# Differential attention in half-sequence units: values stationary against 512 transposed differences in float32, part of the routing on GpSimd

## Chip, cores and metric

One NeuronCore of one Trainium2 chip runs the whole layer. The metric is the device time of one execution in microseconds, the median over the runs.

## The reference

A transformer layer on x of 8 sequences x 1024 tokens x 512 features, in float32. First differential attention, then a routed expert layer with 64 experts; each is added to its input and normalised.

```python
q, k = rope(x @ wq.T), rope(x @ wk.T)        # 8 half-heads of width 64
v = x @ wv.T                                 # 4 heads of width 128
probs = softmax(q @ k.T / 128**-0.5)         # two maps of 1024 x 1024 for each head
diff = probs[:, :, 0] - lam * probs[:, :, 1]
attn = diff @ v
attn = attn * rsqrt(mean(attn**2) + eps) * subln_weight
x = layernorm(x + attn @ wout.T)
scores = softmax(x @ gate_w.T); gate_vals, idx = top_k(scores, 6)
# every expert takes at most 128 (CAP) tokens, in order of the token number
x = layernorm(x + routed_experts(x, idx, gate_vals) + shared_expert(x))
```

## The kernel before

The kernel has four stages that run one after the other: `project` (q, k, v and the rotation), `attend`, `experts` and `finish`. The change touches the first two.
`project` writes q, k and v with both parts to DRAM. For the values ScalarE copies the high part out of PSUM (L200) and VectorE subtracts it to get the low part (`v_low`, L217).

`attend` goes over 256 steps. A step is one head of one batch and one tile of 128 query rows; there are 32 steps a batch, 8 tiles x 4 heads. In every step TensorE makes two score maps of 128 x 1024 (L496, L497: the stationary operand holds both parts of q, the moving ones are the high and low part of k). VectorE takes the negated row maxima (L709). ScalarE takes the exponentials with their sums (L627). VectorE combines both maps into `diff` (L666). TensorE turns `diff` in eight pieces (L507, plain float32 transposes). The turned differences leave PSUM in two parts: the high part by ScalarE (L583), the low part of the first four pieces by VectorE (L672), and for the last four TensorE subtracts the high part inside PSUM by a product with minus the identity (L535), after which ScalarE copies the rest (L602). The value product has the turned differences as the stationary operand, 128 x 128, and the values as the moving one, 256 columns (both parts): 16 matmuls a step (L525, L526). ScalarE copies the half with the low part (L599), VectorE adds the two (L642) and ScalarE squares the result for the norm (L609).

Every engine works in turns, one turn for each step. In one turn TensorE issues scores of step j, the transposes of j-2, one of four pieces of output work, and the value product of j-3. Each engine takes its instructions strictly in this order and waits at semaphores. The two score maps have one buffer each, so scores of step j+1 wait for the exponentials of step j.

The output work of the batch before runs beside it, one tile of 128 tokens in four turns ("pieces", `pe_piece`, L544). Piece 0 turns the normed heads. Piece 1 is the output projection, 12 matmuls of 512 columns, after which VectorE adds x and takes the moments (L684 to L689). GpSimd turns these into scale and shift (L798 to L803, four narrow operations), ScalarE applies them (L575) as the first thing of the turn of piece 2, and TensorE turns the result (L560). Piece 3 is the gate product, 12 matmuls of 64 columns, and the exponentials of the logits (L613). The routing of a tile then takes place in the next four turns, a few small VectorE instructions in each turn (`dve_route`, L711): the six best experts (L726, L730), the mask of hits (L736), its sum over the six (L742, L745), the position in each expert's list by two small matmuls (L541, L542), and the slot number (L754 to L767).

GpSimd's queue for one tile (`pool_tiles`, L792) is strictly in this order: scale and shift of tile n, `pool_hit_pos` of tile n-1 (L814), the norm of the heads of tile n+1 (L780 to L790), and `pool_scatter` of tile n-1 (L816), six indirect DMAs that write token and gate value to the slots. It then waits until they have landed.

After the last batch, a tail of 32 turns has output work alone, 8 tiles. The first batch has no output work beside it. The batches 1 to 7 are one hardware loop.

## Time and profile before

| | |
|---|---|
| median of the timed runs | 3913.32 us (3910.45 and 3916.2) |
| span of the profiled execution | 4009.9 us |
| mean granted clock of TensorE | 0.935 |
| TensorE busy, of the span | 3462.3 us (86%) |
| VectorE busy | 2606.1 us (65%) |
| ScalarE busy | 1993.6 us (50%) |
| GpSimd busy | 1442.9 us (36%) |
| HBM | 375.19 MB read, 185.54 MB written |

The profiled execution is longer than the timed ones. Its timeline is what durations are read from. In it `project` runs from 0 to about 540 us, `attend` from there to about 2560 us, and the experts and the last norm take the rest. A busy share is an average over stages with different limits. An instruction's duration in the profile contains its latency, so that matmuls overlap in the rows; the rate is read from the distance of their starts. In a row of a timeline the last bracket is the idle time of the engine before that instruction and what ended it.

### The profile page before, as it was taken

The numbers are of one execution on the slowest core, as the hardware profiler recorded it, in microseconds if no ns is written. First come the engines' busy times: TensorE is split into PE (matmuls) and PEld (weight loads), VectorE is DVE, ScalarE is ACT, GpSimd is POOL, SyncE is SP. The second block draws the span as 40 slices with busy tenths as digits, with TensorE's granted clock in tenths as the row PEclk, the third lists the DMA queues.
The fourth block names the chain that finished last, engine by engine and source line by source line (L and its number), as shares of the span: only waits on it lengthen the run. The fifth ranks groups of instructions, "written<-read, shape, count | busy, mean of one in ns | idle before, by whom it ended". The sixth has DMA issues, their size and how long they took to land. (4 is left out here: it accounts for less than half of the span.)

```text
span 4009.9 us, 61177 instructions
## 1 busy us (share of the span) xinstructions
PE 3462.3 (86%) x18948; PEld 2965.3 (74%) x18948; DVE 2606.1 (65%) x4553; ACT 1993.6 (50%) x3642; POOL 1442.9 (36%) x1496
## 2 busy tenths in 40 slices
PE   8999969998989989898888985299999999999990
PEld 7888859777777777777777774178887788878870
DVE  6777759888878878888887884244444444444434
ACT  2222228766666666666666661144444344444434
POOL 0000000344343433343443435344454545554442
PEclk9999989999999999999999996599999999999995
DMA  6666675434443433443442421255555555555548
GB/s 241 226 229 225 220 219 115 105 91 104 103 102 88 116 89 87 115 98 78 114 101 78 116 67 48 96 161 153 150 166 166 151 152 156 162 168 144 151 126 342
DMA packets 287215, 563.59 MB, mean 141 GB/s; under 512 B 35744, under 2 KB 102880, under 8 KB 282352
## 3 DMA queue, kind: packets, MB, share of 16 engines
q1 hardware_dynamic: 248624, 493.24, 40.7%
q0 software_dynamic: 36032, 50.60, 7.1%
q10 hardware_dynamic: 2304, 16.78, 1.0%
q8 instruction: 108, 1.77, 0.2%
q14 instruction: 147, 1.20, 0.1%
HBM read 375.19 MB, written 185.54 MB: 140 GB/s over the span
## 5 line engine op out<-in xcount | busy, mean ns | idle before, releaser
L709 DVE TENSOR_REDUCE att_neg_max<-att_ps_s 128x1 f32<-128x1024 f32 x512 | 623.1, 1217 | 181.2 <-PE att_ps_s L497 138.8
L627 ACT ACTIVATE att_prob<-att_ps_s,att_neg_max 128x1024 f32<-128x1024 f32 x512 | 573.6, 1120 | 326.0 <-DVE att_neg_max L709 274.9
L525 PE MATMUL att_ps_o<-att_v,att_diff_hi 128*128 128x256 f32 x2048 | 523.2, 293 | 17.8 <-issue 9.2
L526 PE MATMUL att_ps_o<-att_v,att_diff_lo 128*128 128x256 f32 x2048 | 502.3, 283 | 0.0
L496 PE MATMUL att_ps_s<-att_k_hi,att_q 128*128 128x512 f32 x1024 | 432.6, 423 | 78.0 <-issue 46.0
L1040 POOL TENSOR_TENSOR exp_w_lo<-exp_w_raw,exp_w_hi 128x2816 fp32r<-128x2816 f32 x63 | 401.5, 6373 | 272.9 <-ACT exp_w_hi L1031 272.9
L820 POOL DMA_INDIRECT slots<-att_entry,att_slot x390 | 398.7, 1022 | 248.0 <-DVE att_token L767 131.7
L497 PE MATMUL att_ps_s<-att_k_lo,att_q 128*128 128x512 f32 x1024 | 427.1, 417 | 0.0
L525 PEld LDWEIGHTS att_ps_o<-att_v,att_diff_hi 128*128 128x128 f32 x2048 | 391.9, 191 | 23.9 <-issue 23.4
L526 PEld LDWEIGHTS att_ps_o<-att_v,att_diff_lo 128*128 128x128 f32 x2048 | 393.0, 192 | 0.0
L666 DVE SCALAR_TENSOR_TENSOR att_diff<-att_prob,att_weight 128x1024 f32<-128x1024 f32 x256 | 328.0, 1281 | 5.1
L583 ACT CAST att_diff_hi<-att_ps_t 128x1024 fp32r<-128x1024 f32 x256 | 257.5, 1006 | 101.1 <-remote 94.7
L496 PEld LDWEIGHTS att_ps_s<-att_k_hi,att_q 128*128 128x128 f32 x1024 | 205.0, 200 | 136.4 <-issue 77.8
L507 PEld LDWEIGHTS att_ps_t<-att_ident,att_diff 128*128 128x128 f32 x2048 | 253.7, 148 | 59.2 <-issue 19.7
L507 PE MATMUL att_ps_t<-att_ident,att_diff 128*128 128x128 f32 x2048 | 282.3, 284 | 13.1 <-DVE att_diff L666 6.2
L76 PE MATMUL exp_ps_ab<-exp_x_t_hi,exp_sw_hi 128*128 128x512 f32 x704 | 282.4, 401 | 0.0
L798 POOL TENSOR_TENSOR att_var_eps<-att_mean_var,att_eps_col 128x1 f32<-128x1 f32 x64 | 12.0, 187 | 743.8 <-DVE att_mean_var L689 743.8
L78 PE MATMUL exp_ps_ab<-exp_x_t_hi,exp_sw_lo 128*128 128x512 f32 x704 | 275.5, 391 | 0.0
L77 PE MATMUL exp_ps_ab<-exp_x_t_lo,exp_sw_hi 128*128 128x512 f32 x704 | 275.0, 391 | 0.0
L497 PEld LDWEIGHTS att_ps_s<-att_k_lo,att_q 128*128 128x128 f32 x1024 | 206.7, 202 | 43.6
L1200 DVE TENSOR_TENSOR exp_hid<-exp_ps_ab,exp_silu 128x512 f32<-128x512 f32 x80 | 55.1, 688 | 255.0 <-ACT exp_silu L1169 255.0
L76 PE MATMUL proj_ps_qk<-proj_x_hi,proj_wqk_hi 128*128 128x512 f32 x512 | 200.0, 391 | 14.6 <-DVE proj_wqk_lo L211 14.6
(216 smaller groups left out, 8735.3 us busy)
## 6 DMA issues: line engine op xcount, KB each, us to landing
exp_w_raw<-in_w_t SPq DMA_DIRECT2D x64, 1408.0 KB
att_q<-q_parts SPq DMA_DIRECT2D x132, 256.0 KB
att_k_hi<-k_parts SPq DMA_DIRECT2D x132, 256.0 KB
att_k_lo<-k_parts SPq DMA_DIRECT2D x132, 256.0 KB
att_v<-v_parts SPq DMA_DIRECT2D x33, 1024.0 KB
v_parts<-proj_v_out SPq DMA_DIRECT2D x64, 512.0 KB, 3.4
exp_w_raw<-in_w_t SPq DMA_DIRECT2D x64, 512.0 KB, 3.9
proj_x_raw<-in_x_t SPq DMA_DIRECT2D x17, 1024.0 KB, 7.1
```

The source lines that it names most:

```text
L76: nc.tensor.matmul(out, lhs[0], rhs[0], start=first, stop=False)
L78: return nc.tensor.matmul(out, lhs[1], rhs[0], start=False, stop=last)
L496: nc.tensor.matmul(ps_s[s][:, cols], q_buf[h % 2][:, s, q_cols], k_hi[h % 2][:, s, cols], start=True, stop=False)
L497: last = nc.tensor.matmul(ps_s[s][:, cols], q_buf[h % 2][:, s, q_cols], k_lo[h % 2][:, s, cols], start=False, stop=True)
L507: last = nc.tensor.matmul(ps_t[:, t, :], diff[jl % 2][:, t * P : t * P + P], ident[:], is_transpose=True, start=t <= TILES // 2, stop=t < ...
L525: nc.tensor.matmul(ps_o[:, 0 : 2 * VD], diff_hi[i][:, t, :], v_buf[h % 2][:, t, :], start=t == 0, stop=False)
L526: last = nc.tensor.matmul(ps_o[:, 0 : 2 * VD], diff_lo[i][:, t, :], v_buf[h % 2][:, t, :], start=False, stop=t == TILES - 1)
L627: nc.scalar.activation(prob[s][i][:], ps_s[s][:], ACT.Exp, bias=neg_max[:, s, i : i + 1], accum_out=total).then_inc(exp_done[s], 1)
L666: nc.vector.scalar_tensor_tensor(diff[i][:], prob[1][i][:], weight2[:, i : i + 1], prob[0][i][:], ALU.mult, ALU.add).then_inc(diff_done, 1)
L709: nc.vector.tensor_reduce(neg_max[:, s, i : i + 1], ps_s[s][:], AX.X, ALU.max, negate=True).then_inc(max_done[s], 1)
L820: nc.gpsimd.indirect_dma_start(slots, bass.IndirectOffsetOnAxis(ap=slot[:, c : c + 1], axis=0), entry[:, c, :], None, bounds_check=EXPERTS ...
L1040: engine.tensor_tensor(w13[1][:], w13_raw[:], w13[0][:].bitcast(F32), ALU.subtract).then_inc(w13_lo_done, 1)
```

## The change

- The unit of attention is a "quad": one head of one batch and half of the query rows (four steps of 128 rows). There are 8 quads a batch and again 32 steps. Query loads bring 512 columns and not 1024. Keys are loaded for each quad, so twice as often.
- The turned differences are copied out of PSUM by one ScalarE copy a step into `diff_t`, plain float32. The high and low parts of the differences, their VectorE subtraction, the product with minus the identity and the second ScalarE copy are gone.
- The value product runs once for a quad: eight matmuls, stationary the values (128 keys x 128 features, float32, one part), moving 512 turned differences, float32. They are issued three, two and three in the turns 2, 3 and 0 of the four.
- Its result has features on the partitions. ScalarE copies it out (`out_t`), TensorE turns it back with four transposes, VectorE copies it to `raw`. This takes place in the turn of piece 1.
- `project` writes values in one part; `v_low` is gone.
- Output work of a tile begins 24 turns after the batch's first step (`OUT`), so in the same batch and not one batch later. The tail has 28 turns and holds the output work of 6 tiles.
- In the routing, top values and indices are taken from the exponentials directly, all VectorE work but `pos_k`, the copy of the positions and the running mask sits in the turn of piece 0. The copy of the indices, the three adds that make the mask and all the slot arithmetic are GpSimd instructions.
- GpSimd's order for one tile is now: scale and shift of n, the norm of n+1, `pool_hit_pos` of n-1, `pool_choose` of n, `pool_scatter` of n-1. Two sets of slot buffers take the place of the wait for the landing.

```diff
-    STEPS = HEADS * TILES
+    QT = 4
+    QUADS = 2 * HEADS
+    STEPS = QUADS * QT
+    DIFF, TURN, COPY, VALUE, BACK, SQUARE, OUT, ROUTE = 1, 2, 3, 6, 9, 10, 24, 28
+    VALUE_TILES = [(0, 1, 2), (3, 4), (5, 6, 7)]
...
-        q_buf = [st.sbuf(f"q{i}", [P, 2, SEQ], F32R) for i in range(2)]
+        q_buf = [st.sbuf(f"q{i}", [P, 2, CHUNK], F32R) for i in range(2)]
...
-        v_buf = [st.sbuf(f"v{i}", [P, TILES, 2 * VD], F32R) for i in range(2)]
+        v_buf = [st.sbuf(f"v{i}", [P, TILES, VD]) for i in range(2)]
...
+        diff_t = [st.sbuf(f"diff_t{i}", [P, TILES, CHUNK]) for i in range(2)]
+        out_t = st.sbuf("out_t", [P, CHUNK])
...
+        def pe_turns(pe, b, mode):
+            for jl in turns(mode):
+                piece = jl % QT
+                if live(mode, jl, 0):
+                    pe_scores(pe, b, jl)
+                if piece != 2:
+                    pe_piece(pe, b, jl, mode)
+                if live(mode, jl, TURN):
+                    j = STEPS * b + jl - TURN
+                    pe.wait_ge(diff_done, j + 1)
+                    wait_past(pe, copy_done, j)
+                    for c in range(TILES):
+                        last = nc.tensor.transpose(ps_t[:, c, :], diff[jl % 2][:, c * P : c * P + P], ident[:])
+                    last.then_inc(t_done, 1)
+                if piece == BACK % QT and live(mode, jl, BACK):
...
+                    pe.wait_ge(out_t_done, qn + 1)
+                    for t in range(QT):
+                        last = nc.tensor.transpose(ps_o[:, t * P : t * P + P], out_t[:, t * P : t * P + P], ident[:])
+                    last.then_inc(back_done, 1)
+                i = (jl - VALUE) % QT
+                if i < len(VALUE_TILES) and live(mode, jl, VALUE):
...
+                    for c in VALUE_TILES[i]:
+                        last = nc.tensor.matmul(ps_o[:], v_buf[q % 2][:, c, :], diff_t[q % 2][:, c, :], start=c == 0, stop=c == TILES - 1)
...
+                if piece == 2:
+                    pe_piece(pe, b, jl, mode)
...
+        def act_turns(act, b, mode):
...
+                if piece == BACK % QT and live(mode, jl, BACK):
...
+                    nc.scalar.copy(out_t[:], ps_o[:]).then_inc(out_t_done, 1)
+                if live(mode, jl, COPY):
...
+                    act.wait_ge(t_done, j + 1)
+                    wait_past(act, value_done, qn - 1)
+                    t = (jl - COPY) % QT
+                    nc.scalar.copy(diff_t[q % 2][:, :, t * P : t * P + P], ps_t[:]).then_inc(copy_done, 1)
...
                 if out and piece == 2:
                     act.wait_ge(ln_done, n + 1)
...
                     nc.scalar.activation(x1_buf[k % 2][:], summed[:], ACT.Identity, bias=shift[:], scale=rstd[:]).then_inc(x1_done, 1)
+                if live(mode, jl, 0):
+                    for s in range(2):
+                        exp(act, b, jl, s)
...
         def pool_tiles(pool, b, final):
             for k in range(TILES):
...
                 nc.gpsimd.tensor_tensor(shift[:], neg_mean[:], rstd[:], ALU.mult).then_inc(ln_done, 1)
-                pool_hit_pos(pool, n - 1)
                 if k < TILES - 1:
-                    pool_norm_heads(pool, b - 1, k + 1)
...
+                    pool_norm(pool, n + 1, par, t, STEPS * b + QT * HEADS * par + QT * (HEADS - 1) + t)
...
-                pool_scatter(pool, n - 1)
...
+                if not first:
+                    pool_hit_pos(pool, n - 1)
+                pool_choose(pool, n, k % 2)
+                if not first:
+                    pool_scatter(pool, n - 1, (k - 1) % 2)
...
+        def pool_choose(pool, n, par):
+
+            pool.wait_ge(route_step, ROUTE_STEPS * n + 3)
+            pool.sem_inc(held, 1)
+            nc.gpsimd.tensor_copy(chosen[par][:], top_idx[:, 0:TOPK]).then_inc(chosen_done, 1)
+            pool.wait_ge(hit_step, HIT_STEPS * n + 1)
+            nc.gpsimd.tensor_tensor(hit3[:], hit[:, 0 : TOPK // 2, :], hit[:, TOPK // 2 :, :], ALU.add).then_inc(hit_step, 1)
+            pool.wait_ge(hit_step, HIT_STEPS * n + 2)
+            nc.gpsimd.tensor_tensor(hit2[:], hit3[:, 0, :], hit3[:, 1, :], ALU.add).then_inc(hit_step, 1)
+            pool.wait_ge(hit_step, HIT_STEPS * n + 3)
+            wait_past(pool, seen_done, n)
+            nc.gpsimd.tensor_tensor(mask[:], hit2[:], hit3[:, 2, :], ALU.add).then_inc(mask_done, 1)
...
+            nc.gpsimd.tensor_scalar(over[:], pos_k[:], float(CAP), BIG, ALU.is_ge, ALU.mult).then_inc(slot_step, 1)
+            nc.gpsimd.tensor_scalar(first_slot[:], chosen[par][:], float(CAP), None, ALU.mult).then_inc(slot_step, 1)
+            nc.gpsimd.tensor_copy(entry[par][:, :, 0], token[:].to_broadcast([P, TOPK])).then_inc(token_done, 1)
...
+            nc.gpsimd.tensor_copy(slot[par][:], slot_sum[:]).then_inc(slot_done, 1)
```

In the new order of VectorE, the last routing instruction of the turn of piece 0 makes `hit` (after `diff` of that turn). `pool_choose` waits for it, and `pool_scatter` of the tile before and scale and shift of the next tile are behind `pool_choose` in GpSimd's queue. In the turn of piece 1, VectorE copies `raw` ahead of `diff`, and the sum with x and the moments come after `diff`.

## Rows read from the trace of the kernel before

**Rows 1.** Busy time by stretch: us, busy us of each engine, clock, DMA share
```profile
100.00:500.00 400.00, 400.00 (x1766) 331.23 (x1765) 290.11 (x259) 96.58 (x112) 0.00 (x0) 1.00 0.65 225
...
900.00:1300.00 400.00, 355.49 (x2243) 309.06 (x2243) 331.15 (x708) 258.90 (x555) 161.06 (x214) 0.95 0.41 101
```

**Rows 2.** Timeline of GpSimd: start us, us, engine line op, operands
```profile
748.37 0.19 POOL L798 TENSOR_TENSOR att_var_eps<-att_mean_var,att_eps_col 128x1 f32<-128x1 f32 x1 [10.39 <-DVE att_mean_var L689]
...
949.00 0.19 POOL L798 TENSOR_TENSOR att_var_eps<-att_mean_var,att_eps_col 128x1 f32<-128x1 f32 x1 [10.26 <-DVE att_mean_var L689]
...
2404.85 0.19 POOL L798 TENSOR_TENSOR att_var_eps<-att_mean_var,att_eps_col 128x1 f32<-128x1 f32 x1 [9.10 <-DVE att_mean_var L689]
...
2531.81 0.19 POOL L798 TENSOR_TENSOR att_var_eps<-att_mean_var,att_eps_col 128x1 f32<-128x1 f32 x1 [4.44 <-DVE att_mean_var L689]
...
2556.77 0.97 POOL L820 DMA_INDIRECT slots<-att_entry,att_slot  x1 [0.30 <-issue]
```

**Rows 3.** Timeline of TensorE, parts of two turns
```profile
1485.11 0.39 PE L496 MATMUL att_ps_s<-att_k_hi,att_q 128*128 128x512 f32 x1
...
1486.94 1.03 PE L507 MATMUL att_ps_t<-att_ident,att_diff 128*128 128x128 f32 x8
...
1487.81 0.60 PE L560 MATMUL att_ps_m<-att_ident,att_x 128*128 128x128 f32 x4
...
1488.16 0.36 PE L525 MATMUL att_ps_o<-att_v,att_diff_hi 128*128 128x256 f32 x1
...
1490.15 0.40 PE L535 MATMUL att_ps_t<-att_diff_hi,att_neg_ident 128*128 128x512 f32 x1
...
1493.23 0.28 PE L76 MATMUL att_ps_m<-att_gate_hi,att_x_t_hi 128*128 128x64 f32 x1
...
1494.57 0.36 PE L525 MATMUL att_ps_o<-att_v,att_diff_hi 128*128 128x256 f32 x1
```

**Rows 4.** Group of the row maxima in 590 to 720 us, busy us, mean ns | idle before
```profile
L709 DVE TENSOR_REDUCE att_neg_max<-att_ps_s 128x1 f32<-128x1024 f32 x52 | 63.1, 1214 | 6.9 <-PE att_ps_s L497 6.9
```

**Rows 5.** Timeline of VectorE, two stretches
```profile
1481.83 1.28 DVE L666 SCALAR_TENSOR_TENSOR att_diff<-att_prob,att_weight 128x1024 f32<-128x1024 f32 x1
...
1483.02 0.68 DVE L672 TENSOR_TENSOR att_diff_lo<-att_ps_t,att_diff_hi 128x512 fp32r<-128x512 f32 x1
...
1485.18 0.18 DVE L689 BATCH_NORM_AGGREGATE att_mean_var<-att_stats 128x2 f32<-128x6 f32 x1 [0.15 <-DVE att_stats L686]
...
1499.90 1.22 DVE L709 TENSOR_REDUCE att_neg_max<-att_ps_s 128x1 f32<-128x1024 f32 x1 [2.61 <-remote]
...
1504.26 0.21 DVE L730 FIND_INDEX8 att_top_idx<-att_top_val,att_score 128x8 uint32<-128x64 f32 x1
```

**Rows 6.** Timeline of GpSimd around one tile, and one pause
```profile
1485.45 0.19 POOL L798 TENSOR_TENSOR att_var_eps<-att_mean_var,att_eps_col 128x1 f32<-128x1 f32 x1 [12.24 <-DVE att_mean_var L689]
...
1487.66 1.01 POOL L814 TENSOR_TENSOR att_hit_pos<-att_hit,att_pos 128x384 f32<-128x384 f32 x1 [0.95 <-DVE att_pos L705]
...
1489.27 1.22 POOL L785 TENSOR_TENSOR att_rms_sum<-att_squares,att_eps_mass 128x4 f32<-128x4 f32 x1 [0.17 <-POOL att_eps_mass L782]
...
1494.86 1.08 POOL L820 DMA_INDIRECT slots<-att_entry,att_slot  x1 [1.96 <-DVE att_token L767]
...
1501.55 0.98 POOL L820 DMA_INDIRECT slots<-att_entry,att_slot  x1 [0.30 <-issue]
...
1864.78 0.97 POOL L820 DMA_INDIRECT slots<-att_entry,att_slot  x1 [10.81 <-issue]
```

**Rows 7.** Timeline of ScalarE, three instructions
```profile
1487.65 1.11 ACT L627 ACTIVATE att_prob<-att_ps_s,att_neg_max 128x1024 f32<-128x1024 f32 x1
...
1503.65 1.01 ACT L583 CAST att_diff_hi<-att_ps_t 128x1024 fp32r<-128x1024 f32 x1 [1.20 <-remote]
...
1854.93 1.00 ACT L583 CAST att_diff_hi<-att_ps_t 128x1024 fp32r<-128x1024 f32 x1
```

**Rows 8.** Busy time by stretch, while queries and keys are loaded
```profile
1498.00:1501.00 3.00, 2.11 (x16) 1.70 (x14) 1.09 (x1) 0.28 (x2) 2.39 (x3) 1.00 1.03 200
```

More of the change, by code:

```diff
@@ new lines, in attend, with turns, live, quad @@
+        ROUTE_STEPS, HIT_STEPS, SLOT_STEPS, RMS_STEPS, LN_STEPS = 4, 3, 4, 4, 3
+        SCATTER = DMA * TOPK
+        TILES_ALL = TOKENS // P
+        def turns(mode):
+            return range(ROUTE if mode == "last" else STEPS)
+        def live(mode, jl, lag):
+            return jl >= lag if mode == "first" else jl < lag if mode == "last" else True
+        def quad(b, jl, lag):
+            return QUADS * b + (jl - lag) // QT, (jl - lag) // QT % QUADS
+        def tile(b, jl, lag):
+            at = (jl - lag) // QT
+            return TILES * b + at, at % TILES, TILES // 2 * b + at // 2
@@ new lines, in pe_scores @@
+        def pe_scores(pe, b, jl):
+            q, t, j = jl // QT, jl % QT, STEPS * b + jl
+            if t == 0:
+                pe.wait_ge(qk_in[q % 2], DMA * LOADS_QK * (QUADS // 2 * b + q // 2 + 1))
+            q_cols = slice(t * P, t * P + P)
+            for s in range(2):
+                wait_past(pe, exp_done[s], j)
+                for half in range(2):
+                    cols = slice(half * CHUNK, half * CHUNK + CHUNK)
+                    nc.tensor.matmul(ps_s[s][:, cols], q_buf[q % 2][:, s, q_cols], k_hi[q % 2][:, s, cols], start=True, stop=False)
+                    last = nc.tensor.matmul(ps_s[s][:, cols], q_buf[q % 2][:, s, q_cols], k_lo[q % 2][:, s, cols], start=False, stop=True)
+                last.then_inc(s_done[s], 1)
@@ new lines, in pe_piece @@
+        def pe_piece(pe, b, jl, mode):
+            piece = jl % QT
+            n, k, _ = tile(b, jl, OUT)
+            if piece == 3 and live(mode, jl, ROUTE):
+                pe.wait_ge(mask_done, n)
+                wait_past(pe, seen_done, n - 1)
+                if live(mode, jl, OUT):
+                    pe.wait_ge(xt_lo_done, n + 1)
+                else:
+                    wait_past(pe, score_done, n)
+                nc.tensor.matmul(ps_m[:, POS], before[:], mask[:], start=True, stop=False)
+                nc.tensor.matmul(ps_m[:, POS], ones[:], mask_seen[:], start=False, stop=True).then_inc(pos_done, 1)
+            if not live(mode, jl, OUT):
+                return
@@ L578, in act_turns @@
-                if live[2]:
-                    _, _, _, j2 = of_lag(b, jl, 2)
-                    act.wait_ge(t_done, j2 + 1)
-                    if not (first and jl < 4):
-                        act.wait_ge(o_done, j2 - 1)
-                    nc.scalar.copy(diff_hi[jl % 2][:], ps_t[:]).then_inc(hi_done, 1)
+                if live(mode, jl, 0):
+                    for s in range(2):
+                        exp(act, b, jl, s)
+                if out and piece == 0:
+                    act.wait_ge(at_done, n + 1)
+                    wait_past(act, y_done, n)
+                    nc.scalar.copy(heads_t[0][:], ps_m[:].rearrange("p (h t) -> p h t", t=P)).then_inc(at_hi_done, 1)
@@ L584, in act_turns @@
                 if out and piece == 2:
                     act.wait_ge(xt_done, n + 1)
[L586 removed]
+                    wait_past(act, gate_done, n)
                     nc.scalar.copy(x1_t[0][:], ps_m[:].rearrange("p (h t) -> p h t", t=P)).then_inc(xt_hi_done, 1)
[L588 to L593 removed]
@@ L603, in act_turns @@
-                if live[4]:
-                    bb, h, t, j = of_lag(b, jl, 4)
-                    act.wait_ge(raw_done, j + 1)
-                    if not (first and jl == 4):
-                        act.wait_ge(square_done, j)
-                    par = bb % 2
+                if live(mode, jl, SQUARE):
+                    qn, q = quad(b, jl, SQUARE)
+                    h, par, t = q % HEADS, q // HEADS, (jl - SQUARE) % QT
+                    act.wait_ge(raw_done, qn + 1)
+                    wait_past(act, square_done, STEPS * b + jl - SQUARE)
@@ L879, in _ @@
-                act.wait_ge(weight_step, 1)
-                nc.scalar.copy(wo[0][:], wo_raw[:]).then_inc(setup_act, 1)
-                nc.scalar.copy(gate[0][:], gate_raw[:]).then_inc(setup_act, 1)
+                act_turns(act, 0, "first")
                 with act.Fori(1, BATCH) as b:
-                    act_turns(act, b, True, True, False)
-                act_turns(act, BATCH, False, True, False)
+                    act_turns(act, b, "steady")
+                act_turns(act, BATCH, "last")
```

582 lines of the change are left out of this document (225 added, 357 removed).

## The prediction, made before the changed kernel ran

> **What bounds the kernel now.** I read the busy time by stretch first. `project` is TensorE without a gap, 400 of 400 us [rows 1], VectorE has spare time there. In the steady part of `attend` TensorE has work in 355 of 400 us and VectorE in 331 [rows 1]: two engines near their limit, waiting for each other. So I need the time of one tile (four turns), and what it is made of.
>
> The timeline of GpSimd gives it. The first operation of a tile's scale and shift starts at 748.37 for the first tile and at 949.00 seven tiles later: 28.66 us a tile. Seven batches later it is 2404.85, so 236.6 a batch, of which 8 x 28.66 = 229.3 are tiles and 7.3 the wrap of the loop. The tail then takes (2531.81 - 2404.85) / 7 = 18.1 a tile, and 25.9 us from there to the end of the last scatter at 2557.7 [rows 2]. Without output work a turn takes 130 / 26 = 5.0 us: 52 row maxima, two a turn, in 130 us [rows 4].
>
> What TensorE has to do in one tile follows from starts: scores 1.83 a turn, so 0.229 for a product of 512 columns; transposes 0.87; values 1.99; four more transposes 0.35; gate 1.34 [rows 3]. With the product with minus the identity at 0.229, four turns are 4 x (1.83 + 0.87 + 1.99 + 0.23) = 19.7. The output work adds 12 x 0.229 = 2.75, 1.34 and 2 x 0.35, together 4.8. Sum 24.5 of 28.66: some 4 us a tile are waits.
>
> **TensorE after.** Removed in a tile: 4 x 1.99 and 4 x 0.23, together 8.9. Added: four transposes, 0.35, and eight matmuls of plain float32 with 512 columns, which no row shows. Lower bound: one pass as for the scores, 0.229. I take 0.916: values with one part and differences with one part are only exact enough if the array does the splitting. Then 7.3 are added, and the sum is 24.5 - 8.9 + 0.35 + 7.3 = 23.3.
>
> The Trainium skill's "FP8 and Floating Point Precision", section on TensorE precision notes, says true float32 takes four passes through the array. By it the price is that of my upper bound; by the one pass TensorE would have 17.8 us a tile. No row here can decide.
>
> **The other engines.** VectorE loses the low part (0.60 a turn by the distance to the next start, 0.68 by its row [rows 5]), the add of the halves and the masks. ScalarE loses two copies a turn. Neither is what a turn then waits for by its sum, so I price these removals at nothing themselves. The two waits on TensorE's path they end (scores held by the copy, the product with minus the identity held by the high part) are in the 4 us above. In `project` the removed subtraction lay beside a full TensorE: nothing, about 1 us at the stage's end. The wait of 29 us for the first load gets 0.5 MB less: 2 us.
>
> **GpSimd after, the step that decides.** The queue is in order, so I walk one tile from the moment when VectorE's `hit` is ready (turn of piece 0), called 0. Then, on GpSimd:
> - three adds for the mask, of 192, 64 and 64 columns. 384 columns take 1.0 and a narrow operation 0.19 [rows 6], so 0.6, 0.35, 0.35 with the hand-overs between them: 1.5 with rounding up.
> - seven narrow operations for the slots, 0.2 each: 1.5.
> - six scatters: 1494.86 to 1502.53 [rows 6], 7.7.
> - only then scale and shift of the next tile. That begins at 10.7.
>
> From there to the start of the first exponential it is 1487.65 - 1485.45 = 2.2 [rows 6, 7], the exponential takes 1.1 [rows 7], and at 14.1 TensorE can start scores of the turn of piece 3. Its second map waits for the second exponential, until 15.2, and ends at 16.2. Behind the exponentials ScalarE copies the turned x1 and VectorE makes its low part (0.6 each by the low part in rows 5): 16.4. From there TensorE has work in one piece: gate 1.34, transposes 0.87, two value matmuls 1.83, first score map of the next turn 0.92: 21.4. VectorE needs 1499.90 to 1504.47 = 4.6 from that map's maximum to the index of the top values [rows 5], and 0.5 for `hit`, half of what GpSimd takes for the same 384 columns [rows 6]: 26.5. So 26.5 us a tile.
>
> Without GpSimd in the way, the turn of piece 1 sets the moments: TensorE does scores 1.83, output projection 2.75, transposes 0.87, four back 0.35, so 5.8; VectorE then has `raw`, `diff`, sum, moments. Before, `diff` to the end of the moments was 1481.83 to 1485.36 with the low part in it [rows 5], and `raw` has the size of that part: 3.5. Scale and shift could start at 9.4 and not at 10.7. That would be 25.2 a tile: moving the slots to GpSimd costs 1.3. If the float32 product took one pass, two of them leave the path, but VectorE comes in its place after 0.7: 25.8.
>
> **DMA.** A quad loads 2.5 MB of queries and keys and 0.5 MB of values in one tile's time; before it was 4 MB in two. At the 200 GB/s of such a stretch [rows 8], with 0.75 MB of x in and out, 3.75 MB are 18.8 us of 26.5. The load starts when the scores of the quad before last are done and has over a quad's time to land: hidden.
>
> **A port.** A GpSimd addition of 4 columns took 1.22 us [rows 6] where its like take 0.2; VectorE's `diff`, two inputs from SBUF, is 1.28 long [rows 5]. I read that as a wait for it. In my walk the next `diff` comes at 6.4, behind the masks and slots, so the sum has nothing for it; where it is met it is rival 6. The Trainium skill's "SBUF — State Buffer", section "SBUF: two separate sides", speaks against moving work to GpSimd: a VectorE operation with two SBUF inputs and a GpSimd operation that reads SBUF exclude each other for the whole instruction. The 1.22 us agree with it.
>
> **The sum.** First output tile: 568.1 less 2, some 8 for the slow start, 24 turns at 5.0 - 1.99 - 0.23 + 1.83 + 0.09 = 4.7, so 113, and 13 for turns 24 and 25: 700. Tile 57 is the last with attention beside it: 57 x 26.5 + 7 x 7.3 = 1562 later, 2262. The next, without scores, 24 (before 26 at that place). Five of the tail: a tile's chain there is 18.1; `hit` comes 9.9 after scale and shift begin and GpSimd is busy for 10.7 from there: 20.6, so 103. After the last: 9.9, masks 1.5, slots and scatters 9.2 of tile 62, then positions 1.0 + 0.7, slots 1.5, scatters 7.7: 32. End at 2421 and not 2557.7: 137 us less, in a profiled execution of 4009.9. The timed runs are 3913.3 / 4009.9 = 0.976 of it: -134, so 3780 us.
>
> **The rivals.** All change the time of a tile; one microsecond is 57 x 0.976 = 56 us of the timed run.
> 1. *GpSimd is not late*: 25.2 a tile, 3780 - 72 = 3708. For it: my margin of 1.3 us is thin, two narrow operations less wide would eat half. Against it: six scatters at 1.28 are firm.
> 2. *A copy is held by the scatters.* ScalarE's copy of the turned differences in the turn of piece 0 starts at 1503.65, after 1.2 idle with its releaser unknown, 1.1 after the last scatter's end at 1502.53; in the tile in which the scatters paused for 10.81 us the same copy came without a gap, at 1854.93 [rows 6, 7]. If scatters do hold it, then in the new order the copy of turn 2 (ready at 5.6) is held to 11.8; transposes end at 13.6, three value matmuls at 16.3, turned x1 at 16.7, where scores started at 14.1. A part overlaps with what followed: 2.1 more, 28.6 a tile, 3898: no change.
> 3. *Slower: both copies are held.* The copy of turn 1 starts at 0.7, and the scatters at 3.0. If it comes 2.3 us later it is caught too, the exponentials behind it start at 12.7, scores of the turn of piece 2 at 13.9 and not at 5.9: 8 more, 34.5 a tile, 4228. Against it: it needs those 2.3 us.
> 4. *Slower: the float32 product is dearer.* TensorE's other work is 16.0 a tile, so above (26.5 - 16.0) / 8 = 1.31 it is the bound; the kernel is slower than before from 28.9 a tile, 1.61 each. At 1.83, twice my price, 30.6 a tile: 4010.
> 5. *The loads are not hidden*, if short elements (2 KB for queries, 512 B for values) are slow: needs 1.4 times the 18.8 us. Then the tile is as long as its loads, 27 to 29: 3810 to 3920.
> 6. *Masks or slots meet a `diff`* once in a tile, as the addition of 1.22 us did: 1.2 more, 27.7 a tile, 3847. Against it: `hit` stands right behind a `diff`, with a turn to the next.
>
> **How the numbers follow.** Forecast 0.40, rival 1 0.19, rival 2 0.20, rival 3 0.07, rival 4 0.06, rival 5 0.04, rival 6 0.04. The forecast's own range is 3730 to 3835 (25.7 to 27.5 a tile). The range for 8 in 10 reaches from 3700, rival 1, to 3910, just above rival 2; it leaves out rivals 3 and 4, 0.13, and the edges of others, some 0.07. More than 2% (below 3835, above 3992, about what a measurement can tell from no change) comes out faster in rival 1, nearly all of the forecast and a part of rival 5, 0.60; slower in 3 and 4, 0.13; the rest 0.27.
>
> **What would show it.** Right: the first operation of scale and shift comes 26.5 us apart, straight behind the sixth scatter, and its idle time has no VectorE releaser; float32 value matmuls start 0.92 apart; the x1 operation of ScalarE waits for GpSimd some 3 us a tile; TensorE is busy for about 88% of that stretch. Rival 1: GpSimd idle before scale and shift. Rival 2 or 3: the copy into `diff_t` idle with an unknown releaser while scatters run. Rival 4: value matmuls over 1.3 apart. Rival 5: scores waiting for a DMA. Wrong altogether: a time below 3680, which only a TensorE with less to do and no queue before it could give, or above 4030.

## The result: slower, and the profile after

The changed kernel takes 4152.7 us (4129.4 and 4176.1), against 3913.3: ratio 1.061, 95% interval 1.047 to 1.076. I had forecast 3780 and a range from 3700 to 3910. The span of the profiled execution is 4174.4, 164.5 more than before; here it is close to the timed runs, before it was 97 us above them.

**Stretches.** `project` and the experts are unchanged, `attend` is not. Columns as in [rows 1]: us, busy us of PE, PEld, DVE, ACT, POOL, granted clock, DMA share, GB/s.

```profile
100.00:500.00 400.00, 400.00 (x1767) 331.20 (x1766) 260.83 (x211) 96.88 (x110) 0.00 (x0) 1.00 0.57 193
900.00:1300.00 400.00, 349.49 (x1502) 247.60 (x1501) 261.27 (x463) 219.48 (x438) 188.84 (x348) 0.87 0.55 128
1300.00:1700.00 400.00, 351.32 (x1396) 249.65 (x1395) 239.54 (x422) 200.77 (x400) 176.93 (x313) 0.80 0.51 118
```

TensorE looks as busy as before (349 of 400), with a third fewer matmul records. A part of that busy time is work at the lower clock: 0.87 and then 0.80, where [rows 1] had 0.95. VectorE fell from 331 to 261 and is no limit. DMA is at 0.55.

**The tile.** Scale and shift (now L707), timeline of GpSimd, as in [rows 2]:

```profile
697.22 0.19 POOL L707 TENSOR_TENSOR att_var_eps<-att_mean_var,att_eps_col 128x1 f32<-128x1 f32 x1 [17.72 <-DVE att_mean_var L662]
722.28 0.19 POOL L707 TENSOR_TENSOR att_var_eps<-att_mean_var,att_eps_col 128x1 f32<-128x1 f32 x1 [8.06 <-DVE att_mean_var L662]
750.42 0.85 POOL L707 TENSOR_TENSOR att_var_eps<-att_mean_var,att_eps_col 128x1 f32<-128x1 f32 x1
780.47 0.85 POOL L707 TENSOR_TENSOR att_var_eps<-att_mean_var,att_eps_col 128x1 f32<-128x1 f32 x1
...
1680.48 0.94 POOL L707 TENSOR_TENSOR att_var_eps<-att_mean_var,att_eps_col 128x1 f32<-128x1 f32 x1
1714.62 0.86 POOL L707 TENSOR_TENSOR att_var_eps<-att_mean_var,att_eps_col 128x1 f32<-128x1 f32 x1
...
2561.18 0.84 POOL L707 TENSOR_TENSOR att_var_eps<-att_mean_var,att_eps_col 128x1 f32<-128x1 f32 x1
```

The first four rows hold the case in short. Up to the second row no scatter stands ahead of scale and shift: 25.06 us, and GpSimd is idle until the moments come. Up to the third there are six: 28.14, no idle time. The next distance is 30.05, and later it is 34.14. Over 57 tiles the mean is (2561.18 - 697.22) / 57 = 32.7.

**What stands ahead of scale and shift.** The same timeline, from the end of VectorE's `hit` (1265.66):

```profile
1265.74 0.60 POOL L740 TENSOR_TENSOR att_hit<-att_hit 128x192 f32<-128x192 f32 x1 [1.76 <-DVE att_hit L643]
...
1268.74 0.19 POOL L764 CAST att_slot<-att_slot_sum 128x6 int32<-128x6 f32 x1 [0.17 <-POOL att_slot_sum L761]
1269.79 1.10 POOL L770 DMA_INDIRECT slots<-att_entry,att_slot  x1 [0.86 <-POOL att_slot L764]
1271.19 0.98 POOL L770 DMA_INDIRECT slots<-att_entry,att_slot  x1 [0.30 <-issue]
1272.48 1.80 POOL L770 DMA_INDIRECT slots<-att_entry,att_slot  x1 [0.30 <-issue]
...
1277.14 0.97 POOL L770 DMA_INDIRECT slots<-att_entry,att_slot  x1 [0.30 <-issue]
1278.12 0.85 POOL L707 TENSOR_TENSOR att_var_eps<-att_mean_var,att_eps_col 128x1 f32<-128x1 f32 x1
```

From `hit` to scale and shift pass 12.5 us; I had 10.7. The moments had been ready for 3.0 us (rows of VectorE and ScalarE in the same tile; L565 is ScalarE's operation that makes x1, the normed sum):

```profile
1272.16 1.28 DVE L639 SCALAR_TENSOR_TENSOR att_diff<-att_prob,att_weight 128x1024 f32<-128x1024 f32 x1
1274.95 0.18 DVE L662 BATCH_NORM_AGGREGATE att_mean_var<-att_stats 128x2 f32<-128x6 f32 x1 [0.18 <-DVE att_stats L658]
1277.64 1.28 DVE L639 SCALAR_TENSOR_TENSOR att_diff<-att_prob,att_weight 128x1024 f32<-128x1024 f32 x1
1280.08 0.81 ACT L565 ACTIVATE att_x<-att_summed,att_shift,att_rstd 128x512 f32<-128x512 f32 x1 [7.95 <-POOL att_shift L712]
```

**What TensorE does about it.** Its timeline in that tile, and in one of the longer ones:

```profile
1274.42 2.74 PE L483 MATMUL att_ps_o<-att_diff_t,att_v 128*128 128x512 f32 x6
1281.03 1.09 PE L532 MATMUL att_ps_m<-att_ident,att_x 128*128 128x128 f32 x4 [3.87 <-ACT att_x L565]
1282.03 0.79 PE L498 MATMUL att_ps_s<-att_k_hi,att_q 128*128 128x512 f32 x1
1282.62 0.63 PE L499 MATMUL att_ps_s<-att_k_lo,att_q 128*128 128x512 f32 x1
1283.05 0.63 PE L498 MATMUL att_ps_s<-att_k_hi,att_q 128*128 128x512 f32 x1
...
1649.37 1.09 PE L532 MATMUL att_ps_m<-att_ident,att_x 128*128 128x128 f32 x4 [4.01 <-ACT att_x L565]
...
1658.42 3.62 PE L483 MATMUL att_ps_o<-att_diff_t,att_v 128*128 128x512 f32 x4
1661.06 1.42 PE L498 MATMUL att_ps_s<-att_k_hi,att_q 128*128 128x512 f32 x1
...
1662.78 0.39 PE L499 MATMUL att_ps_s<-att_k_lo,att_q 128*128 128x512 f32 x1
```

After the last three value matmuls TensorE stands for some 4 us, waiting for x1, and then the scores come 0.43 apart where [rows 3] had 0.23. Busy time by stretch of the same two tiles, and of the stretch with which the experiments are compared:

```profile
1281.00:1287.00 6.00, 5.97 (x21) 4.58 (x21) 3.04 (x5) 4.96 (x10) 2.25 (x3) 0.51 0.42 134
1287.00:1306.00 19.00, 18.88 (x97) 14.02 (x97) 13.82 (x29) 11.20 (x23) 8.35 (x16) 1.00 0.79 166
...
1649.00:1662.00 13.00, 12.63 (x39) 9.18 (x40) 4.99 (x9) 8.21 (x18) 3.06 (x3) 0.50 0.64 164
1662.00:1676.00 14.00, 13.85 (x68) 10.42 (x67) 10.39 (x20) 8.39 (x16) 6.05 (x14) 0.99 0.59 131
...
1500.00:2200.00 700.00, 616.09 (x2443) 437.80 (x2444) 423.18 (x743) 355.67 (x705) 311.25 (x559) 0.81 0.50 117
```

The lower level of the clock (1.2 GHz) is granted for 6 us behind the one gap and for 13 behind the other; the rest of the tile runs at 2.4. The tile that began at 1249.81 had a gap of only 0.99 and full clock and took 28.3; these take 30.6 and 34.1. In 6 us at half rate 3 us of work are done, and in 13 us 6.5, so 3 and 6.5 us can be lost; the tiles are 2.3 and 5.8 longer. The Trainium skill's "TensorE: Matmul & The Clock Gate", section on HAM oscillation, describes a matmul kernel in which a wait in each step of a loop sends the clock back to the lower level again and again; this trace agrees, with 0.80 over 1300 to 1700.

So the theory before the experiments: GpSimd's queue makes x1 late; TensorE stands for 4 us; the stall costs a second time, by the clock behind it. The rivals: the float32 value product is what costs, by its length or by drawing the clock down on its own; or GpSimd's work costs wherever it stands.

### The profile page after: what moved, and what is told of

Read it like the earlier page. It is cut to its first block and busy times, and to the rows that moved or that the text cites. A ratio compares the mean times of both kernels' runs of the same rounds, so it can differ in the third digit from the quotient of the medians.

```text
span 4174.4 us, 53729 instructions
## 1 busy us (share of the span) xinstructions
PE 3593.0 (86%) x15874; PEld 2785.7 (67%) x15874; DVE 2274.4 (54%) x3428; ACT 1864.7 (45%) x3194; POOL 1631.2 (39%) x2191
## 5 line engine op out<-in xcount | busy, mean ns | idle before, releaser
L498 PE MATMUL att_ps_s<-att_k_hi,att_q 128*128 128x512 f32 x1024 | 544.9, 532 | 35.4 <-DVE att_neg_lam L836 27.4
L483 PE MATMUL att_ps_o<-att_diff_t,att_v 128*128 128x512 f32 x1024 | 542.3, 667 | 0.9 <-DVE att_raw L635 0.9
L770 POOL DMA_INDIRECT slots<-att_entry,att_slot x384 | 422.8, 1101 | 155.9 <-issue 105.0
L499 PE MATMUL att_ps_s<-att_k_lo,att_q 128*128 128x512 f32 x1024 | 454.6, 444 | 0.0
L483 PEld LDWEIGHTS att_ps_o<-att_diff_t,att_v 128*128 128x128 f32 x1024 | 201.6, 214 | 176.6 <-issue 175.5
L467 PE MATMUL att_ps_t<-att_ident,att_diff 128*128 128x128 f32 x2048 | 307.9, 299 | 12.2 <-DVE att_diff L639 2.7
L556 ACT COPY att_diff_t<-att_ps_t 128x1024 f32<-128x1024 f32 x256 | 259.3, 1013 | 85.6 <-PE att_ps_t L467 56.3
L467 PEld LDWEIGHTS att_ps_t<-att_ident,att_diff 128*128 128x128 f32 x2048 | 256.4, 154 | 50.1 <-DVE att_diff L639 35.3
L532 PE MATMUL att_ps_m<-att_ident,att_x 128*128 128x128 f32 x256 | 66.4, 411 | 250.0 <-ACT att_x L565 250.0
L565 ACT ACTIVATE att_x<-att_summed,att_shift,att_rstd 128x512 f32<-128x512 f32 x64 | 52.0, 812 | 509.0 <-POOL att_shift L712 509.0
L532 PEld LDWEIGHTS att_ps_m<-att_ident,att_x 128*128 128x128 f32 x256 | 43.7, 209 | 299.5 <-issue 299.5
```

Of the source, the lines that this page charges most:

```text
L467: last = nc.tensor.transpose(ps_t[:, c, :], diff[jl % 2][:, c * P : c * P + P], ident[:])
L483: last = nc.tensor.matmul(ps_o[:], v_buf[q % 2][:, c, :], diff_t[q % 2][:, c, :], start=c == 0, stop=c == TILES - 1)
L498: nc.tensor.matmul(ps_s[s][:, cols], q_buf[q % 2][:, s, q_cols], k_hi[q % 2][:, s, cols], start=True, stop=False)
L499: last = nc.tensor.matmul(ps_s[s][:, cols], q_buf[q % 2][:, s, q_cols], k_lo[q % 2][:, s, cols], start=False, stop=True)
L770: nc.gpsimd.indirect_dma_start(slots, bass.IndirectOffsetOnAxis(ap=slot[par][:, c : c + 1], axis=0), entry[par][:, c, :], None, bounds_che ...
```

## The experiments

Line numbers are those of each kernel; they are up to five higher than those of the changed one. All ratios are to the kernel before. Clocks are those of the stretch from 1500 to 2200 us, sums of waits those from 1350 to 2300 (for experiment 10 from 1500 to 2200).

**1. The scatters one tile later** (`e1_scatter_late`). GpSimd's order is scale and shift, heads, slots and scatters of two tiles ago, `hit_pos`, masks:

```diff
+                late = not (isinstance(b, int) and n < 2)
+                if late:
+                    pool_scatter(pool, n - 2, k % 2)
                 if not first:
                     pool_hit_pos(pool, n - 1)
+                if late:
+                    pool.wait_ge(scattered[k % 2], SCATTER * (TILES // 2 * b + (k - 2) // 2 + 1))
+                    pool.sem_inc(entry_free, 1)
                 pool_choose(pool, n, k % 2)
-                if not first:
-                    pool_scatter(pool, n - 1, (k - 1) % 2)
...
```

> All work is done; the six scatters of a tile and their slots are issued one cycle later on GpSimd, behind the scale of the heads (L699), so that the scale and shift (L707) follows the masks directly. Theory (queue): in the changed kernel L707 starts 3.0 us after VectorE's moments, behind the sixth scatter; here it starts right behind the moments. TensorE's idle time before L532 falls from 3.7 us a tile to under 1.5, its granted clock in 1500:2200 rises from 0.81 to 0.95 or more, a tile takes 25 to 26.5 us and not 30.7 to 34.1, and the time is 3700 to 3850. Rival A (the float32 value product lowers the clock by itself): the tile gets only the 3.0 us, the clock stays at 0.80 to 0.85, time 3950 to 4000. Rival B (the float32 product or the DMA is the bound): idle time moves elsewhere, time 4050 to 4150.

4346.9 us, ratio 1.113 (1.109 to 1.117): the slowest of all, 35.3 us a tile. No expectation named this. Scale and shift does follow the moments (GpSimd is idle for 9.7 us ahead of it), and something else is late:

```profile
1690.11 1.04 POOL L732 TENSOR_TENSOR att_hit_pos<-att_hit,att_pos 128x384 f32<-128x384 f32 x1
1696.81 0.23 DVE L628 TENSOR_SCALAR att_entry<-att_top_val,att_score_inv 128x6 f32<-128x6 f32 x1 [8.31 <-POOLq L725]
...
1696.99 0.23 POOL L738 CAST att_chosen<-att_top_idx 128x6 f32<-128x6 uint32 x1 [5.84 <-DMA slots<-att_entry,att_slot]
```

Entries have two buffers. VectorE may write the next one when the scatters of two tiles ago have landed, and I had just put those scatters in front of it. VectorE stands for 8.3 us in the middle of its turn. In the changed kernel's own order that release had been free.

**2. TensorE kept busy in the gap** (`e2_filler`), with FILL = 15:

```diff
                 pe.wait_ge(sum_done, n + 1)
+                for _ in range(FILL):
+                    nc.tensor.matmul(ps_m[:], heads_t[0][:, 0, :], wo[0][:, 0, :], start=True, stop=True)
                 pe.wait_ge(x1_done, n + 1)
```

> All work is done, the order is that of the changed kernel; TensorE gets 15 products of 512 columns (3.4 us at full clock) whose result nobody reads, in front of its wait for x1 (L532). The wait stays, the idleness goes. Theory (clock): the granted clock in 1500:2200 rises from 0.81 to 0.95 or more and the tile falls to the 28.3 us of the one tile in which the clock did not drop, so the time is 3860 to 3920. Rival A (the float32 product lowers the clock, not the gap): clock stays near 0.80, tile 33 to 34, time 4150 or more. Rival C (the wait alone is the cost, the clock is a by-product of waiting): clock up, tile unchanged, 4130 to 4170.

3964.4 us, ratio 1.014 (1.011 to 1.018). Busy time by stretch, timeline of TensorE:

```profile
1500.00:2200.00 700.00, 669.03 (x3210) 478.28 (x3210) 486.56 (x866) 410.66 (x823) 361.18 (x650) 1.00 0.61 137
```

```profile
1711.34 4.01 PE L532 MATMUL att_ps_m<-att_wo_hi,att_heads_t_hi 128*128 128x512 f32 x15
1715.69 0.66 PE L535 MATMUL att_ps_m<-att_ident,att_x 128*128 128x128 f32 x4 [0.33 <-ACT att_x L568]
```

The wait for x1 is no shorter than it was, 4.3 us, but filled with useless work, and the kernel is 188 us faster than the changed one: clock 1.00 and not 0.81, 29.0 us a tile and not 32.7. With more work on TensorE and the same float32 products, the clock stays up. So the product does not draw it down; the gap does. The time is some 45 us above my window. Most tiles take 28.8 and not 28.3, which is 28 us of it; the rest is not explained by this run. It is also still 51 us above the kernel before: giving back the clock does not make the change a gain while the queue stands.

**3. The value product in one pass** (`e3_one_pass`): `v_buf` and `diff_t` in float32r.

```diff
-        v_buf = [st.sbuf(f"v{i}", [P, TILES, VD]) for i in range(2)]
+        v_buf = [st.sbuf(f"v{i}", [P, TILES, VD], F32R) for i in range(2)]
...
-        diff_t = [st.sbuf(f"diff_t{i}", [P, TILES, CHUNK]) for i in range(2)]
+        diff_t = [st.sbuf(f"diff_t{i}", [P, TILES, CHUNK], F32R) for i in range(2)]
...
```

> Leaves out precision: values and turned differences are float32r, so a value matmul takes one record of 0.23 us and not 0.87; TensorE has 5.1 us a tile less to do. Everything else as in the changed kernel. Theory (queue): only the two value matmuls in the piece that waits for x1 leave the chain, 1.3 us; the idle time before L532 gets longer and the clock still drops, to half for a stretch in each tile; tile 29 to 33 us, time 3950 to 4100. Rival B (the float32 product is what made the kernel slower): 57 x 5.1 = 290 us and more come back, time 3800 to 3860, which is below the kernel before.

3982.6 us, ratio 1.016 (1.010 to 1.022). TensorE has 5.1 us a tile less, the tile gets 3.1 shorter (29.6), and TensorE's wait before L532 grows from 3.8 to 5.8 us. Waits, total us, times, longest: first the changed kernel, then this one.

```profile
PE att_ps_m L532 <- ACT att_x L565: 106.6, 28, 4.1
...
PE att_ps_m L532 <- ACT att_x L565: 186.1, 32, 6.0
```

The clock is 0.84. A cheaper product does not repair the kernel: it gives back 170 of the 239 us and leaves the kernel 1 to 2% slower than before. It gives more than the 1.3 us of the two value matmuls on the chain. One reason can be that these had run at half rate in the longer tiles (the row of 3.62 us above, four records); this is argued and not shown by a run of its own.

**4. One scatter, not six** (`e4_one_scatter`): five of the six are left out, nothing else moves.

```diff
-        SCATTER = DMA * TOPK
+        SCATTER = DMA
...
-            for c in range(TOPK):
+            for c in range(1):
```

> Leaves out five of the six scatters of each tile (5 of 6 routed entries are not written); masks and slots stay where they are. GpSimd's queue ahead of scale and shift gets 6.6 us shorter. Theory (queue): L707 starts behind the moments as in e1, TensorE's gap before L532 is under 1.5 us, clock 0.95 or more, time within 50 us of e1. If e1 is much slower than this, the scatters cost something in their new place too (a shared port); if both stay above 4000, the queue of scatters is not the cause.

3737.5 us, ratio 0.956 (0.953 to 0.959). Scale and shift comes 25.2 to 25.5 us apart (the first at 1007.80), with GpSimd idle ahead of it:

```profile
1033.32 0.18 POOL L707 TENSOR_TENSOR att_var_eps<-att_mean_var,att_eps_col 128x1 f32<-128x1 f32 x1 [4.32 <-DVE att_mean_var L662]
1058.53 0.18 POOL L707 TENSOR_TENSOR att_var_eps<-att_mean_var,att_eps_col 128x1 f32<-128x1 f32 x1 [4.33 <-DVE att_mean_var L662]
...
1500.00:2200.00 700.00, 660.57 (x3177) 458.87 (x3176) 540.33 (x973) 454.44 (x915) 249.22 (x611) 1.00 0.65 149
```

Five issues in GpSimd's queue, some 6.6 us, and the writes that they start are gone, and 415 us came back. TensorE has all its work, the float32 products among it. The experts get incomplete lists here, but their part of the time is the same: 1439 us from the last scatter to the end, and 1442 in the changed kernel. Whether it is the issues or the writes is told by experiment 8, which has all six.

**5. Four entry buffers** (`e5_late_free`): experiment 1 with `range(4)` for `entry`, and the release taken from the scatters of four tiles ago.

> All work is done. As e1 (slots and scatters one cycle later, behind the scale of the heads), but with four buffers for the entries and not two, so that VectorE's write of the scores (L628) does not have to wait for scatters just issued. Theory: e1 did not fail by its order but by that wait: VectorE stood 216 us in 26 tiles at L628, 8.3 a tile, until the scatters' data had landed. Without it scale and shift comes behind the moments, the clock is at full rate, a tile takes 25.0 us as in e4, and the time is 3730 to 3790, below the kernel before by 3 to 5%. Rival (the scatters cost something in the new place too: a port shared with VectorE, or hit_pos late behind them): tile 27 and more, 3850 and more.

3956.9 us, ratio 1.012 (1.009 to 1.014). 390 us better than experiment 1, so its reading was right, and still 1% slower than before: my theory fell here and the part of the rival that names a late `hit_pos` held. The block of some 10 us now stands before `hit_pos`, which VectorE waits for before it may overwrite `hit`:

```profile
1709.09 0.97 POOL L770 DMA_INDIRECT slots<-att_entry,att_slot  x1 [0.30 <-issue]
1710.07 1.01 POOL L732 TENSOR_TENSOR att_hit_pos<-att_hit,att_pos 128x384 f32<-128x384 f32 x1
1711.18 0.56 DVE L643 TENSOR_TENSOR att_hit<-att_iota,att_top_idx 128x384 f32<-128x384 f32 x1 [5.81 <-POOL att_hit_pos L732]
...
1712.12 0.68 DVE L651 TENSOR_TENSOR att_heads_t_lo<-att_ps_m,att_heads_t_hi 128x512 fp32r<-128x512 f32 x1
1712.95 0.77 PE L76 MATMUL att_ps_m<-att_wo_hi,att_heads_t_hi 128*128 128x512 f32 x1 [5.33 <-DVE att_heads_t_lo L651]
```

Behind `hit` stands the low part of the heads, and behind that TensorE, 5.3 us. So the 10 us block made something late in both places in which it was tried as a block.

**6. The same in one pass** (`e6_late_one_pass`): experiments 5 and 3 together.

> Leaves out precision: e5 with values and turned differences in float32r, 0.23 us for a value matmul and not 0.87. In the changed kernel this took 3982.6 of 4152.7, with the clock still falling (e3). Theory: with the queue out of the way TensorE is busy for 94% of e5, so 5.1 us a tile less work on it leaves VectorE and the chain through x1 as the limit: tile 22.5 to 24 us, time 3620 to 3710. If nothing is gained against e5, the float32 product was hidden there; if the whole 5.1 us come off (below 3500), TensorE's sum alone set the tile.

3980.3 us, ratio 1.018 (1.015 to 1.020): 23 us slower than experiment 5, although TensorE has less to do. My numbers had assumed a queue that was out of the way, and it was not. TensorE's gap before the output projection went from 80.4 us in 29 tiles to 126.4 in 29, the clock from 0.97 to 0.88. It says the same as experiment 3: what TensorE saves goes into its gaps.

**7. Half of the filling** (`e7_half_filler`): experiment 2 with FILL = 8.

> All work is done. As e2, with 8 products in front of the wait for x1 (1.8 us) and not 15, so that about 2 us of idle time stay in each tile. If any idleness of that kind lowers the clock for a stretch, the clock is near 0.8 to 0.9 and the time 4050 to 4150. If only the longer gap of 4 us does, the clock is 0.95 or more and the time within 30 us of e2 (3964).

4006.4 us, ratio 1.026 (1.022 to 1.029), clock 0.96, 29.8 us a tile, with 56.4 us of waiting in 28 tiles left (2.0 each). It lies between my two cases: most tiles lose little of the clock with a gap of 2 us, some lose more (starts at 1090.09 and 1123.55, 33.5 apart). So the second cost is not in proportion to the gap: from 0.4 to 2.0 us of waiting (experiments 2 and 7) the time grows by 42 us, from 2.0 to 3.8 (the changed kernel) by 146.

**8 and 9. The scatters split over GpSimd's free stretches** (`e8_split_2_4`, `e9_split_3_3`). Two (three) of the scatters stay behind the slots, the others follow one tile later behind the heads; four entry buffers.

```diff
                 if not (isinstance(b, int) and n < 2):
-                    pool.wait_ge(scattered[k % 2], SCATTER * (TILES // 2 * b + (k - 2) // 2 + 1))
-                    pool.sem_inc(entry_free, 1)
+                    pool_send(k % 2, (k - 2) % 4, range(EARLY, TOPK))
                 if not first:
                     pool_hit_pos(pool, n - 1)
                 pool_choose(pool, n, k % 2)
+                if not (isinstance(b, int) and n < 3):
+                    pool.wait_ge(scattered[(k - 1) % 2], SCATTER * (TILES // 2 * b + (k - 3) // 2 + 1))
                 if not first:
-                    pool_scatter(pool, n - 1, (k - 1) % 2)
+                    pool.sem_inc(entry_free, 1)
+                    pool_slots(pool, n - 1, (k - 1) % 2, (k - 1) % 4)
+                    pool_send((k - 1) % 2, (k - 1) % 4, range(EARLY))
```

> All work is done. e5 moved the whole wait: slots and six scatters between the scale of the heads and hit_pos (L732) made hit_pos late, and VectorE stood 92 us in 29 tiles at the next hit (L643). In the kernel with one scatter GpSimd has two free stretches in a tile: 4.2 us before scale and shift (158.6 in 38) and 4.1 + 3.1 before hit_pos and chosen (154.9 and 118.7 in 38 and 39). Here two scatters follow the slots after the masks, and four of them come one cycle later behind the scale of the heads, before hit_pos; four entry buffers. Theory (a queue with gaps that must be filled, not a block that must be moved): scale and shift follows the moments within 1 us, hit waits for nothing, clock 0.98 or more, tile 25.0 to 26, time 3740 to 3800, 3 to 4.5% below the kernel before. Rival (scatters cost VectorE or GpSimd time through a shared port wherever they stand): tile 27 or more at full clock, 3850 or more.

> As e8, with three scatters behind the slots and three a cycle later. Three take 3.8 us and the free stretch before scale and shift is 4.2 with one scatter in it already, so two more fit with 1.7 left: theory, within 20 us of e8. If the limit is thinner (a scatter held 0.8 us by VectorE's diff, as in the changed kernel), scale and shift is late by up to 1 us and the time is 30 to 60 us above e8.

3754.7 and 3754.5 us, both ratio 0.960 (0.958 to 0.962, and 0.957 to 0.963). All the work is done, in 4% less time than the kernel before takes and 10% less than the changed one. GpSimd in one tile of `e8_split_2_4`:

```profile
1642.20 1.08 POOL L775 DMA_INDIRECT slots<-att_entry,att_slot  x1 [0.85 <-POOL att_slot L767]
1643.59 0.97 POOL L775 DMA_INDIRECT slots<-att_entry,att_slot  x1 [0.30 <-issue]
1647.64 0.18 POOL L708 TENSOR_TENSOR att_var_eps<-att_mean_var,att_eps_col 128x1 f32<-128x1 f32 x1 [3.09 <-DVE att_mean_var L663]
...
1652.42 1.07 POOL L775 DMA_INDIRECT slots<-att_entry,att_slot  x1 [0.17 <-issue]
...
1656.33 1.43 POOL L775 DMA_INDIRECT slots<-att_entry,att_slot  x1 [0.30 <-issue]
1657.76 1.05 POOL L735 TENSOR_TENSOR att_hit_pos<-att_hit,att_pos 128x384 f32<-128x384 f32 x1
1661.42 0.19 POOL L741 CAST att_chosen<-att_top_idx 128x6 f32<-128x6 uint32 x1 [2.61 <-DVE att_entry L629]
```

The block is cut where the engine would wait: 3.09 us of idle time are left before scale and shift and 2.61 before `chosen`. Its busy time by stretch:

```profile
1500.00:2200.00 700.00, 660.42 (x3186) 459.10 (x3185) 541.91 (x975) 454.43 (x915) 399.09 (x752) 1.00 0.66 149
```

The full price of five more scatters a tile against experiment 4 is 17 us in the whole kernel, and even that is not in the 57 tiles, which take 25.6 us in both; it lies in the tail, where the last scatter ends 19 us later. So it was the place of the issues that cost time, and neither their number nor their writes. The rival that they cost something wherever they stand is refuted, though a single one is longer beside VectorE (1.43).

**10. The split, in one pass** (`e10_split_one_pass`): experiments 8 and 3 together.

> Leaves out precision: e8 with values and turned differences in float32r. Theory: where GpSimd is not late TensorE is the engine that the tile is made of (661 of 700 us busy with one scatter), so here the four passes cost something: of 5.1 us a tile less on TensorE 1 to 3 come off, time 3570 to 3700. If it is no faster than e8, the price of the float32 product was never on the path.

3711.5 us, ratio 0.949 (0.946 to 0.952): 43 us less than experiment 8, under 1 us a tile of the 5.1 us taken from TensorE. I had given 3570 to 3700. TensorE is busy for 557 of 700 us, waits 2.5 us a tile for x1 (72.3 in 29) and 1.3 for the low part of the heads (34.3 in 26), and its clock is 0.91. How much of the missing gain is the chain and how much the clock isn't told apart by this run.

## Why the prediction was wrong

**What held.** Scale and shift comes "straight behind the sixth scatter", and x1 waits for it. The float32 price, taken as the upper bound 0.916, is 0.87: each value matmul has two records, 1024 in `attend` for 512 matmuls, and six are 2.74 us, of which one alone has a row of 0.59, so they start 0.43 apart. The Trainium skill's "FP8 and Floating Point Precision", section on TensorE precision notes (four passes), agrees in length: 0.87 is near four times 0.23. Rival 4 (1.31 and more) is out. Rivals 2 and 3 are out: the copy into `diff_t` starts at 1266.11 and 1271.11 beside masks and scatters without a wait that scatters could explain. Rival 5 is out: the DMA share is 0.51 to 0.55 and no start of scores in the steady part waits for a load. The first tile is at 697.2 (forecast 700), and from tile 57 to the last scatter pass 167.5 us (forecast 159). Even the walk without GpSimd in the way was right: 25.2, and 25.06, 25.3 and 25.3 were measured in the first tile and in experiments 4 and 8, where scale and shift starts 9.6 us after `hit` (I had 9.4). One sign came out by chance: TensorE is busy for 87% of the stretch (I had 88), but in part with work at half rate. Another did not: x1 waits 7.9 us for GpSimd (220.7 in 28), and not some 3.

**First wrong step, the size of the queue.** "only then scale and shift of the next tile. That begins at 10.7", counted from `hit`; it is 12.5. Of the difference 0.86 is a gap between the slots' rounding and the first scatter, which I did not see as a term although a scatter needs its slots finished; 0.6 is scatters, 8.3 and not 7.7, since one that meets VectorE's `diff` takes 1.80; the rest is in the masks and slots. My margin over the moments was 1.3 us, so an error of 1.8 more than doubled the lateness, to 3.0. What I priced as rival 6 at 0.04, a wait for `diff`, is thus in most tiles, but at the scatters and at scale and shift, not at the masks. Of the 64 scale and shifts 52 begin beside a `diff` and take 0.84 to 0.94 us, the other 12 take 0.19 to 0.23. 52 of the 384 scatters take over 1.4 us; they begin beside a `diff` and end 0.84 us behind its end, where the others take 0.97 to 1.3. The Trainium skill's "SBUF — State Buffer", section "SBUF: two separate sides", says that a VectorE operation with two SBUF inputs and a GpSimd operation that reads SBUF exclude each other. The scale and shift shown agrees: it ends at 1278.97, right behind that `diff` (1278.92). This makes the tile 28.3 and not 26.5: 57 x 1.8 = 103 us.

**Second wrong step, the clock.** I took a stall for its length. In "From there TensorE has work in one piece", up to 21.4, the prices are those of full clock; behind a gap of 4 us they are up to twice that. [rows 1] showed a clock of 0.95 in the kernel before, and I did not look at what the engine had done before it fell there. From 28.3 the tile goes to 32.7 in the mean: 57 x 4.4 = 251 us. That is the larger error. It does not turn faster into slower by itself: my sum with the first error alone would read 3880, but experiment 2, with that queue and the clock at 1.00, was measured at 3964, 51 us above the kernel before. Some 40 us of the 84 between them are its tile, 29.0 and not 28.3; the third point below is large enough for the rest, which no run takes apart. The sum in the span: +103, +251, and -51 for the loop's wraps, which cost next to nothing here (at one, 33.17 and then 28.31 us where the neighbours are 30.7), together 303; the 57 tiles are 302 us longer than forecast.

**Third, a matter of scale.** I multiplied the gain by 0.976, but the profiled execution of before was itself 97 us above its timed runs, and that of after only 22 above its own. The change in the traces (+164.5) and in the times (+239) therefore differ by 75 us. So of the 373 us between 3780 and 4153, 302 are tiles that are longer than forecast, and this is about the rest. A forecast of the time after that starts from the span before carries that in it. The last scatter is followed by 1448 us in the trace before and by 1430 to 1444 in all others, and `project` is as long in all, so most of the 97 us probably lies in `attend` of that one execution; no run shows where.

**Where the gain went.** The change is worth something once it is not in its own way: 3755 against 3913. The time lay in a queue of an engine, GpSimd, that was busy for only 854 of the 2020 us from 540 to 2560.

**What stays open.** Where in detail experiment 6 loses 23 us against experiment 5. Why the lower clock lasts 6 us behind one gap and 13 behind another of the same length; the kernel goes from one kind of tile to the other at 902.61, back, and again at 1339.48. And what the masks and slots on GpSimd bring by themselves: no run took them back to VectorE.

## What to carry to other kernels

Work that is moved to a lightly used in-order engine must be laid into the places where that engine waits, in pieces of their size, and each piece's releases (a buffer freed, a next input read) must be followed to who waits for them: as one block it was harmful in both places tried, cut in two it cost 17 us. When a forecast holds a stall of TensorE in every round of a loop, price work behind it at half clock too: here 3.8 us of it did so in nearly every tile, and 2.0 us in a part of them. And a margin of 1.3 us under a queue of 10 us is no margin: list its gaps between instructions as terms.

## What the runs showed of the hardware

A stall of TensorE costs twice, and filling it with useless products gave back 188 us of 4153: in these kernels 3.8 us of idle time in each tile goes with a mean granted clock of 0.81, 2.0 us with 0.96, and 0.4 us with 1.00. With a one-pass product, TensorE less busy (557 of 700 us) and waiting 2.5 us, it was 0.91. A cheaper TensorE instruction can so be worth almost nothing: 5.1 us less of work a tile gave 3.1 us in experiment 3, under 1 us in experiment 10, and a loss of 23 us in the whole kernel in experiment 6.

A GpSimd instruction, the issue of an indirect DMA among them, that began beside VectorE's `diff` was held until after it: 1.8 us and not 0.97 for an issue, 0.85 and not 0.19 for one column.
